# Second attention: maximum rows in bf16 sent by DMA instead of a broadcast cast, and the parts of x made two half units earlier

## The reference

```
x = x + tanh(g_xattn[0]) * L0_xattn(layernorm(x), ctx)       # one head, softmax over queries
x = x + tanh(g_ffn[0])   * L0_ffn(layernorm(x))              # gated landmark experts, exp and log
x = x + tanh(g_xattn[1]) * L1_xattn(ctx, ctx, layernorm(x))  # 16 heads of 16, softmax over 77 keys
x = x + tanh(g_ffn[1])   * L1_ffn(layernorm(x))              # self attention, 16 heads, masked by class
```

## Time and profile before

| | us |
|---|---|
| median of 3 runs | 1420.08 (1419.99 to 1422.82) |
| the profiled execution | 1424.06 |
| its span, first to last instruction | 1422.3 |
| busy: TensorE, VectorE, ScalarE, GpSimd | 1264.7, 1044.8, 854.3, 160.5 |
| mean granted TensorE clock | 0.942 |

### The profile page before, as it was taken

The page is one execution under the profiler, slowest core; times in us unless marked ns, Lnnn a source line. Parts: engine busy times, 40 slices in busy tenths (PEclk is TensorE's granted clock), DMA queues, the critical chain, the costliest instruction groups (busy, mean ns, idle before and its releaser), DMA issues.

```text
span 1422.3 us, 26541 instructions
## 1 busy us (share of the span) xinstructions
PE 1264.7 (89%) x10690; PEld 590.5 (42%) x10690; DVE 1044.8 (73%) x1563; ACT 854.3 (60%) x1432; POOL 160.5 (11%) x139
## 2 busy tenths in 40 slices
PE   4898974899899899948899999999999999999988
PEld 3566662454455755514433233232322333233237
DVE  4897494666664756545699999999999999999802
ACT  2233472666665155511287877887887787887871
POOL 2220021110600223310600000000000000000000
PEclk8977985999999999978799999999999999999999
DMA  5000026444450013340524443323443323443003
GB/s 177 24 1 14 1 29 111 95 85 89 90 90 2 0 67 133 134 94 11 82 50 69 82 79 57 75 54 64 82 81 62 67 56 63 82 81 48 2 1 118
DMA packets 78825, 92.56 MB, mean 65 GB/s; under 512 B 15210, under 2 KB 53356, under 8 KB 78704
## 3 DMA queue, kind: packets, MB, share of 16 engines
q1 hardware_dynamic: 78704, 90.87, 31.6%
HBM read 67.02 MB, written 23.80 MB: 64 GB/s over the span
## 4 chain that ended last, share of the span: by engine, by line
PE 58%; DVE 28%; ACT 7%; issue 4%; DMA 1%; SPq 1%; POOL 1%; DVEq 0%; ACTq 0%; POOLq 0%
DVE sm L1971 18%; PE ps L1460 9%; PE ps L1451 8%; PE ps L1432 6%; PE ps L1351 4%; ACT W L964 3%; PE ps L1216 2%; PE ps L1250 2%; PE ps L1570 2%; PE ps L1167 2%; PE ps L1358 2%; PE ps L1241 2%; PE ps L1299 1%; PE ps L1442 1%; PE ps L1387 1%
## 5 line engine op out<-in xcount | busy, mean ns | idle before, releaser
L1971 DVE TENSOR_REDUCE sm<-ps 128x1 f32<-128x1024 f32 x512 | 599.8, 1218 | 33.1 <-PE ps L1432 29.8
L964 ACT ACTIVATE W<-ps 128x512 f32<-128x512 f32 x1024 | 534.8, 604 | 140.2 <-PE ps L1460 136.3
L1460 PE MATMUL ps<-R 99*32 99x512 bf16 x4096 | 318.5, 383 | 6.2 <-ACT W L964 3.2
L1451 PE MATMUL ps<-W,R 128*32 128x512 f32 x2048 | 266.4, 596 | 0.7 <-ACT W L964 0.7
L1460 PEld LDWEIGHTS ps<-R 99*32 99x32 bf16 x4096 | 86.2, 94 | 225.4 <-ACT W L964 168.5
L882 ACT CAST R<-ps 4x2048 bf16<-4x2048 f32 x32 | 59.5, 1858 | 80.7 <-PE ps L1216 80.7
L1776 DVE TENSOR_REDUCE small<-ps 128x4 f32<-128x308 f32 x128 | 60.9, 477 | 62.6 <-PE ps L1205 62.2
L1432 PE MATMUL ps<-R 50*128 50x512 bf16 x512 | 89.2, 389 | 15.6 <-DVE sm L1971 12.9
L1432 PE MATMUL ps<-KM,R 50*128 50x512 bf16 x512 | 87.2, 384 | 9.6 <-DVE sm L1971 6.6
L1451 PEld LDWEIGHTS ps<-W,R 128*32 128x32 f32 x2048 | 63.2, 111 | 42.5 <-ACT W L964 1.4
L765 POOL COPY R<-R 128x512 f32<-128x512 f32 x16 | 10.3, 644 | 591.7 <-PE ps L1451 591.7
(11 more groups left out here) (258 smaller groups left out, 1587.1 us busy)
## 6 DMA issues: line engine op xcount, KB each, us to landing
R<-x_parts SPq DMA_DIRECT2D x96, 128.0 KB, 4.8
R<-q_parts SPq DMA_DIRECT2D x192, 64.0 KB
R<-q_parts SPq DMA_DIRECT2D x96, 128.0 KB
R<-k_parts SPq DMA_DIRECT2D x96, 128.0 KB
x_parts<-R SPq DMA_DIRECT2D x8, 768.0 KB, 4.1
q_parts<-R SPq DMA_DIRECT2D x24, 256.0 KB, 2.6
k_parts<-R SPq DMA_DIRECT2D x24, 256.0 KB, 2.6
X<-in_x SPq DMA_DIRECT2D x4, 1024.0 KB, 9.8
```

The costliest lines, as they stand in the source:

```text
L964: act.activation(PR[:, s % 2, h, :], third_bank("score", 64 * u + n), ACT.Exp, scale=0.25).then_inc(s_sfree, 1)
L1451: mm = pe.matmul(bank(7)[32 * h:32 * h + 32, :], VST[j][:, k, h, :], PR[:, s % 2, h, :], start=(k == 0), stop=(k == TB - 1))
L1460: mm = pe.matmul(o[32 * c:32 * c + 32, :], KST[j][0:MAX_ROW + 1, h, t:t + 32], QST[j][0:MAX_ROW + 1, h, 512 * (s // 8):512 * (s // 8) + 51 ...
L1971: dve.tensor_reduce(MX[:, half, h, q:q + 1], bank(2 * ((p + 1) % 2), 2), AX, ALU.max).then_inc(s_tfree, 1)
```

## The change

Four things change in the second attention.

1. The negated maxima are written in bf16 (Mn), and `max_transposes1` multiplies them by the bf16 identity instead of the float32 one.
2. ScalarE copies the four rows once, as bf16, to `mrow1` (4 rows of 512, two buffers). Then, after waiting for its own copy, it issues four DMAs from its own queue. DMA j brings row j to the one row 96 of the query stack, in head j's columns. The stacks have 97 rows instead of 100, and the key stack has ones in row 96 (one memset in place of four copies). `scores1(m)` waits for the DMAs of its half unit (`s_mrl`), no longer for ScalarE's cast.
3. On TensorE `max_transposes1(m + 2)` comes before `out_transposes1(m - 2)`.
4. The halves of the batches 2 and 3 are made in half units 6 to 9 and 14 to 17 instead of 8 to 11 and 16 to 19, and the chunks that they need are normalised earlier.

```diff
-        SR1 = SR + 4
+        SR1 = SR + 1
...
+        mrow1 = R2f[SR:SR + 4, 5434:5946].bitcast(BF16).rearrange("p (u n) -> p u n", u=2)
...
-        Mn = small[:, 464:528].rearrange("p (u q j) -> p u q j", u=2, q=8)
+        Mn = small[:, 464:496].bitcast(BF16).rearrange("p (u q j) -> p u q j", u=2, q=8)
...
+        HALVES = {max(0, 8 * (i // 4) - 2) + i % 4: FIRST + i for i in range(12)}
+        CHUNKS = {0: 3, 4: 4, 6: 5, 12: 6, 14: 7}
+
         def half_in(m):
-            return FIRST + 4 * (m // 8) + m % 8 if m % 8 < 4 and m // 8 + 1 < B else None
+            return HALVES.get(m)
...
             def max_rows1(m):
                 act.wait_ge(s_mt, m + 1)
+                if m >= 2:
+                    act.wait_ge(s_mrl[m % 2], 64 * (m // 2))
+                act.copy(mrow1[:, m % 2], bank(2)[SR:SR + 4, :]).then_inc(s_mrc, 1)
                 if m >= 6:
                     act.wait_ge(s_sc, 4 * (m - 5))
-                act.copy(Xs[m // 2 % 3][SR:SR1, :, 512 * (m % 2):512 * (m % 2) + 512],
-                         bank(2)[SR:SR1, :].unsqueeze(1).to_broadcast([4, 4, 512])).then_inc(s_mrc, 1)
+                act.wait_ge(s_mrc, m + 1)
+                for j in range(4):
+                    act.dma_start(Xs[m // 2 % 3][SR:SR1, j, 512 * (m % 2):512 * (m % 2) + 512],
+                                  mrow1[j:j + 1, m % 2]).then_inc(s_mrl[m % 2], 16)
...
-                    mm = pe.matmul(bank(2)[SR:SR1, P * i:P * i + P], Mn[:, m // 2 % 2, 4 * (m % 2) + i, :],
-                                   identF[:, :], start=True, stop=True)
+                    mm = pe.matmul(bank(2)[SR:SR + 4, P * i:P * i + P], Mn[:, m // 2 % 2, 4 * (m % 2) + i, :],
+                                   identB[:, :], start=True, stop=True)
...
-                pe.wait_ge(s_mrc, m + 1)
+                pe.wait_ge(s_mrl[m % 2], 64 * (m // 2 + 1))
...
+                if m + 2 < 2 * UNITS:
+                    max_transposes1(m + 2)
                 if m >= 2:
                     out_transposes1(m - 2)
-                if m + 2 < 2 * UNITS:
-                    max_transposes1(m + 2)
...
-            for g in range(4):
-                sel = dve.tensor_copy(K1s[SR:SR1, 4 * g:4 * g + 4, :],
-                                      identB[SR:SR1, SR:SR1].unsqueeze(2).to_broadcast([4, 4, B * KX]))
-            sel.then_inc(s_mk1, 1)
+            dve.memset(K1s[SR:SR1, :, :], 1.0).then_inc(s_mk1, 1)
...
-                c = 2 * (m // 8) + {0: 3, 6: 4}.get(m % 8, NC)
-                if c < NC:
-                    ln_chunks(2, [c], lambda c: None)
+                if m in CHUNKS:
+                    ln_chunks(2, [CHUNKS[m]], lambda c: None)
```

More of the change, by code:

```diff
@@ L247, in build_program @@
         s_mrc = sem("max1_rows")
+        s_mrl = [sem(f"max1_rows_loaded{n}") for n in range(2)]
         s_sc = sem("scores1")
```

## The result

The changed kernel takes 1471.03 us in the median of four runs (1462.90 to 1477.99), the kernel before beside it 1420.03 (1418.20 to 1422.82). The ratio is 1.0355, with a 95% interval from 1.0297 to 1.0413: slower by 3.6%, where 1402.5 was forecast with a range from 1389 to 1421.

The account below looks back on a forecast made before the run. Bound: a ring through ScalarE and TensorE, 5.74 us per plain half unit, TensorE alone close at 5.52. Gains 19.3 - 2 + 1.4 = 18.7, rounded down to 17.7, from 1420.08 gave 1402.5 us; range 1389 to 1421.

Parts of the forecast that it names:

- The price of the issue: ScalarE's cost per row DMA issue, paid four times per half unit: 0.457 us each, bounds 0.30 and 0.67.
- rival two: Issues at about 0.62 us leave the plain half unit as long as before: 1420, no change; chance 0.07.
- The ring: Plain half unit's dependency loop through ScalarE and TensorE: 5.74 us before, 3.24 plus four issues after, 5.07.
- TensorE alone: TensorE's own work in a plain half unit: 5.52 us before, 4.78 after max transposes save 0.74.
- A part's half unit: Half unit also making part of x for the next batch: 7.17 us before, gaining 0.66, about 6.5 after.
- rival three: Rows land late in SBUF, TensorE waits: slower, 1439 at 6 us landing; chance 0.17 together with dear issues.
- the dear issue's 1425: Each row DMA issue at 0.67 us lengthens 29 spacings by 0.18: 5 us slower; within the 0.17 for slower.
- Late rows: Landing of row DMAs before the scores: 3.0 us allowed, 1.6 expected in the median, costed at nothing.
- The bias episode: VectorE's negation held beside GpSimd's bias after the last part: 6.9 us lost before; change counted 0, plus or minus 4.
- Parts earlier: Parts of x two half units earlier: buys nothing, charged 2 us for two crowded half units on VectorE.
- At the start: Two max transposes at low clock as the stage starts: +1.4 us gain, bounds 0 and 2.8.
- One (cheap issues, 1390): Issues on ScalarE at or below 0.38 us make TensorE the bound, plain spacing 4.78: 1389.5 us; chance 0.26.

Follow-up runs that it names:

- e1: Changed kernel without the four row DMAs, so scores are not shifted by the maxima; 1404.38 us, 0.9882 of the kernel before.
- e3: Kernel before with only the bf16 max transposes and their place before the output transposes, one broadcast cast kept; 1406.11 us, ratio 0.9879.
- e13: e1 with ScalarE's waits and 128 DMAs put back, into columns nobody reads; TensorE waits for the copy alone; 1466.19 us, ratio 1.0316.
- e9: Changed kernel with SyncE issuing the row DMAs, its six stack loads per unit split, three behind each half unit's rows; 1461.78 us, ratio 1.0215.
- e12: e9 with the maxima negated by the transposing product instead of by VectorE; 1463.83 us, ratio 1.0289.
- e11: Kernel before with the parts of x and the chunks two half units earlier, nothing else; 1419.71 us, ratio 1.0003.
- e6: e3 without VectorE's negation: maxima reduced straight to bf16, transposes multiply by a negated identity; 1393.06 us, ratio 0.9812.
- e10: e6 with the parts of x and the chunks two half units earlier; 1386.85 us, ratio 0.9766.
- e5: Changed kernel without VectorE's negation: maxima reduced straight to bf16, transposes multiply by a negated identity; 1453.91 us, ratio 1.0234.
- e2: Changed kernel with two of the four row DMAs per half unit, for heads 0 and 1; 1424.61 us, ratio 1.0003.
- e14: e10 with five useless ScalarE copies ahead of the exponentials of half unit 24, once; 1390.43 us, ratio 0.9777.
- e16: e10 with ten useless ScalarE copies ahead of the exponentials of half unit 24, once; 1397.33 us, ratio 0.9838.
- e17: e10 with four useless ScalarE copies in each of half units 22, 24, 26 and 28; 1401.15 us, ratio 0.9863.
- e7: Changed kernel with ScalarE's cast of the part of x placed between the row copy and the four DMA issues; 1460.02 us, ratio 1.0285.
- the best version: e10: e6 with the parts of x and the chunks two half units earlier; 1386.85 us, 33 us under the kernel before.
- e8: e5 with unread filler products on TensorE, four in plain half units and twelve in those with a part; 1459.81 us, ratio 1.0284.

## Why the prediction was wrong

- **The price of the issue** is the step that failed in the sum. I took 0.457 from SP's (SyncE's) loads of the same number and size of pieces and called that row nearest. It measured 0.61 in the median, 0.78 in the half unit at 251 and up to 1.62, and 0.59 on SyncE itself. Those loads have their source in DRAM and these in SBUF; no run varied the source alone, so that this is the reason stays open. The bounds of 0.30 and 0.67 held the median, and by rival two's condition (d about 0.62) the plain half unit came out as it says: 5.74 measured, 5.74 before, 5.07 forecast.
- **The ring was the right model.** With 0.61 in it, 3.24 + 4 x 0.61 = 5.68, and 5.72 to 5.85 was measured. TensorE alone was put at 4.78 and is 4.67 (e1, e3). The transposes saved what was said.
- **A part's half unit** gains the same 0.66, I said, so 6.5. It takes 7.34 at best. More important, the wait at the third score grew from 1.00 to as much as 2.93 us. I had this ring written out, the four issues ahead of the part's cast in it, and did not ask what an idle time of that length does to TensorE.
- **The clock was in no step and no rival**, and this is the step that failed for the size and the sign of the loss: an idle time of TensorE was priced at its own length. The half units with products at 1.2 GHz cost 37.7 us in the loop, longer waits in them included, and the low clock is in the 8.1 behind it. The earlier trace rows had shown it: behind a wait of TensorE the granted clock was 0.57, and I booked that as an episode of the bias, not as the price of a wait. The far bound for rival three, 1439 at a landing of 6 us, and the dear issue's 1425 are both ring arithmetic at full clock, and the result lies above all of them.
- **Late rows** were a minor term in the changed kernel: 4.8 us of waits, landing 2.9 in the median against 3.0 allowed. e13 shows that the loss does not need them. Whether they would be the bound with a free ScalarE isn't shown: in e9 and e12 TensorE waited for the displaced stack loads, and 0.3 and 0.4 us for rows.
- **The bias episode**, put at 0 with 4 us either way, was too narrow. The negation took 3.85 us here (TensorE's wait 1.81, behind a 2.49 us wait for rows) and 9.18 in e3. I had weighed one GpSimd instruction. The Trainium skill (SBUF — State Buffer, "SBUF: two separate sides", list "Reading the diagram") says that, of a GpSimd instruction and a VectorE one that needs the shared ports, whichever starts first holds them for the whole instruction. A row of 9.18 us, begun 0.1 us after the third of the 4.48 us instructions and ended behind the fourth, shows that VectorE can lose the next turn as well.
- **Parts earlier** cost nothing that shows (e11). In the traces of the fast kernels (e6, e10) waits for a batch's first stack are shorter with them, which the prediction had put at nothing; the times don't separate it. At the start the first spacing is 3.79 for 5.07, 1.3 of the 1.4 us foreseen, but it begins 1.2 us later.
- **The rivals.** One (cheap issues, 1390) has no support: no issue was under 0.50. Two had the right price, and by the sums above would have held to within some 5 us had the clock not fallen. Three had the right side by the wrong mechanism.

What stays open is how long the clock stays low. In the changed kernel from 403 to 447, in e9 from 452, in e5 from 384 and in e2 from 367 on, TensorE is full for three to seven half units near 8.8 us and isn't given its clock back, while in e14 it has it back after one. A longer stall makes it longer (e16, one half unit of 8.8 more), and recurring ones only sometimes (e17); neither reaches five. What ends such a stretch isn't settled by these runs. Nor is what else brings a fall: the clock was low for some 3 us from 337 in e10 and for some 7 from 260 in e7, where TensorE's waits just before were 0.46 to 0.73 us.

## What to carry to other kernels

Price a DMA issue as work of the engine that issues it, and put it in the ring with what stands behind it on that engine: here four issues of 0.61 us to save a 1.27 us difference in a cast that two free edits had already hidden. Measure the edits of a bundle one by one before costing the dear one; here two of them alone (e3) bring 14 of the best version's 33 us. Where an edit moves issues to another queue, look at which of that queue's own transfers now leaves later (e9). And where TensorE is nearly full, an added wait of 2 us or more may have to be charged with a half unit at half clock as well: here that happened behind most such waits, and not behind all.

## What was not expected of the hardware

- Behind one idle time of 2.79 us TensorE worked at half the granted clock for about 6 us (e14), behind one of 6.04 for about 15 (e16); waits of 1.63 and 2.20 us were followed by the lower clock in e2 and e9, one of 2.14 in e17 and one of 2.22 in e8 were not.
- TensorE, busy without a gap, stayed at 1.2 GHz for 70 us in e2 (361 to 431), 47 in the changed kernel (403.5 to 450.5) and 40 in e9 (446 to 486).
- An SBUF to SBUF DMA of 1 KB costs the issuing engine 0.50 to 1.62 us, 0.59 to 0.61 in the median, on ScalarE as on SyncE, and lands after 1.6 us at best and 7.0 to 7.6 at worst.
- A negation of 16 columns on VectorE was held for 9.18 us beside GpSimd, but reductions from PSUM that write bf16 kept their 0.48 us beside the same bias instructions (e6, e10), and so did the normalisation with one input in PSUM and one in SBUF (0.42 us).
